# Widening the inverted softmax denominators on ScalarE instead of VectorE

## What is computed

```
x1 = x  + proj( attention( qkv(group_norm(x)) ) ) + bias          # layer 0
y  = x1 + (attention([x1, emb] Wq, [x1, emb] Wk, x1 Wv)) Wout + b # layer 1
attention: softmax(q k / 8) v  per head and image
```

## Time and profile before

| | |
|---|---|
| median of 3 runs | 4526.37 us (4523.8 to 4527.9) |
| the profiled execution: time | 4527.92 us |
| the profiled execution: span, first to last instruction | 4526.1 us |
| granted TensorE clock, mean of the span | 0.991 of full speed |
| TensorE busy | 4293.3 us, 95% |
| VectorE, ScalarE, GpSimd busy | 71%, 61%, 32% |
| one block in the steady part, 3089.54 to 3124.92 | 35.38 us, of which TensorE is busy 33.99 |

### The profile page before, as it was taken

The page is one execution under the profiler, slowest core; times in us unless marked ns, Lnnn a source line. Parts: engine busy times, 40 slices in busy tenths (PEclk is TensorE's granted clock), DMA queues, the critical chain, the costliest instruction groups (busy, mean ns, idle before and its releaser), DMA issues. The chain is left out here.

```text
span 4526.1 us, 87274 instructions
## 1 busy us (share of the span) xinstructions
PE 4293.3 (95%) x32280; PEld 2523.6 (56%) x32280; DVE 3200.0 (71%) x2892; ACT 2747.3 (61%) x2885; POOL 1455.2 (32%) x584
## 2 busy tenths in 40 slices
PE   7998999999999999998999979999999999999999
PEld 4554555555555555554555545555555555555545
DVE  4223888888888888887433348888888888888862
ACT  1112777777777777776011128777777777777750
POOL 0000444444444444444100004444444444444430
PEclk9999999999999999999999999999999999999999
DMA  5334111211112111120444441211112111111216
GB/s 196 128 128 133 24 53 33 64 33 50 42 44 54 36 47 38 49 50 30 163 149 167 139 115 26 65 33 50 42 44 53 36 47 38 49 42 45 61 32 213
DMA packets 234733, 321.69 MB, mean 71 GB/s; under 512 B 12080, under 2 KB 221104, under 8 KB 233648
## 3 DMA queue, kind: packets, MB, share of 16 engines
q1 hardware_dynamic: 214512, 292.54, 22.3%
q10 hardware_dynamic: 20160, 28.32, 1.7%
HBM read 188.69 MB, written 132.12 MB: 71 GB/s over the span
## 5 line engine op out<-in xcount | busy, mean ns | idle before, releaser
L619 POOL TENSOR_TENSOR prob<-prob,mx 128x1056 f32<-128x1056 f32 x576 | 1434.2, 2490 | 2907.7 <-DVE prob L619 2906.3
L766 ACT ACTIVATE prob<-psum_att 128x1152 f32<-128x1152 f32 x1152 | 1294.1, 1132 | 817.1 <-DVE run L851 635.2
L708 PE MATMUL psum_att<-qst,kst 128*128 128x384 f32 x6912 | 1416.7, 348 | 49.2 <-DMA kst<-qk_scratch 27.6
L779 ACT ACTIVATE prob<-prob 128x1152 f32<-128x1152 f32 x1152 | 1288.1, 1163 | 17.3 <-POOL prob L619 17.3
L708 PEld LDWEIGHTS psum_att<-qst,kst 128*128 128x128 f32 x6912 | 1182.4, 190 | 177.9 <-issue 144.8
L721 PE MATMUL psum_att<-prob,vst 128*32 128x384 f32 x13824 | 1234.2, 490 | 4.7 <-ACT prob L779 2.9
L851 DVE TENSOR_TENSOR run<-psum_att,run 128x1152 f32<-128x1152 f32 x768 | 1013.2, 1349 | 222.3 <-PE psum_att L708 222.1
L619 DVE TENSOR_TENSOR prob<-prob,mx 128x1248 f32<-128x1248 f32 x576 | 996.1, 1730 | 155.8 <-ACT mx L773 155.8
L721 PEld LDWEIGHTS psum_att<-prob,vst 128*32 128x32 f32 x13824 | 391.7, 109 | 593.4 <-issue 593.2
L730 PE MATMUL psum_att<-prob,const_sb 128*32 128x384 f32 x6912 | 663.2, 486 | 0.0
L317 PE MATMUL psum<-xc_l,wq 128*128 128x384 f32 x1536 | 505.1, 490 | 10.4 <-DVE hl_l L422 5.3
(11 more groups left out here) (55 smaller groups left out, 1498.0 us busy)
## 6 DMA issues: line engine op xcount, KB each, us to landing
qk_scratch<-hl_l SPq DMA_DIRECT2D x48, 1536.0 KB, 5.6
qst<-qk_scratch SPq DMA_DIRECT2D x192, 384.0 KB, 5.5
kst<-qk_scratch SPq DMA_DIRECT2D x192, 192.0 KB, 3.3
v_scratch<-vo_l SPq DMA_DIRECT2D x24, 768.0 KB, 3.5
vst<-v_scratch SPq DMA_DIRECT2D x96, 192.0 KB, 2.5
att_scratch<-ob ACTq DMA_DIRECT2D x96, 192.0 KB, 1.9
attc_l<-att_scratch SPq DMA_DIRECT2D x24, 768.0 KB, 5.3
x_sb<-in_x SPq DMA_DIRECT2D x8, 1152.0 KB, 14.2
```

Source lines behind the costliest of these rows:

```text
L619: return engine.tensor_tensor(x, x, m, ALU.subtract)
L708: mm = nc.tensor.matmul(psum[:, 3 * e + k, 0:CH], kst[:, e, (3 * c + k) * P:(3 * c + k + 1) * P], qst[par][:, 2 * w + e, :], start=(w == 0 ...
L766: nc.scalar.activation(chunk_of(par, c, e), s_bank(e), ACT.Copy).then_inc(copied, 1)
L779: nc.scalar.activation(x, x, ACT.Exp, scale=SCALE).then_inc(exp_done, 1)
```

## The change

The copy of the inverted denominators into `dwide` is taken from VectorE's `invert` and becomes an activation on ScalarE, `widen(t)`, which does the same (`ACT.Copy` of the operand that repeats each inverse 64 times) and signals the same semaphore. It stands at the end of ScalarE's group 2 (`DEN_TURN_AT`), behind both copies of scores and both exponentials of that group. It waits for `inverted` and, like the copy before it, for the last `spread`. The flag `POOL_BEHIND`, which was True, goes, and its wait is unconditional.

```diff
--- before.py
+++ after.py
@@ -28,7 +28,6 @@
 GN_EPS = 1e-5
 NORM_STEPS = 10
 SHIFT_DVE = 208
-POOL_BEHIND = True
 SHIFT_LAG, EXP_LAG, PV_LAG = 7, 9, 10
 PV_COLS = 32
 DEN_PAIRS = [[0], [1, 2], [3], [4, 5], [6], [7, 8]]
@@ -786,6 +785,14 @@
                 nc.scalar.activation(pvr[:, :], pv_bank, ACT.Copy).then_inc(pv_copied, 1)
                 nc.scalar.activation(den[:, :], den_bank, ACT.Copy).then_inc(den_copied, 1)
 
+            def widen(t):
+                act.wait_ge(inverted, t + 1)
+                if not before(t, 1):
+                    act.wait_ge(spread, t)
+                nc.scalar.activation(dwide.rearrange("p r (e i) -> p r e i", e=2),
+                                     dcol[:, :, :].unsqueeze(3).broadcast_to([P, 3, 2, D]), ACT.Copy)\
+                    .then_inc(widened, 1)
+
             def store(t, par):
                 pair = t // JB
                 pair_row, j_off = (pair % PAIRS) * P, (pair // PAIRS) * HW + (t % JB) * CH
@@ -807,6 +814,8 @@
                             copy_max(t - 1, 1 - par, e)
                     if live(te):
                         exponential(te, pe_, ce, 1)
+                    if c == DEN_TURN_AT and not before(t, 3) and live(t - 3):
+                        widen(t - 3)
                     if c == STORE_AT and not before(t, 3) and live(t - 3):
                         store(t - 3, 1 - par)
 
@@ -823,8 +832,7 @@
                         if c == 0:
                             pool.wait_ge(mx_ready, unit(t, 1))
                         pool.wait_ge(copied, slot(t, c, 1))
-                        if POOL_BEHIND:
-                            pool.wait_ge(dve_shifted, group(t, c))
+                        pool.wait_ge(dve_shifted, group(t, c))
                         shift_part(nc.gpsimd, par, c, SHIFT_DVE, CH).then_inc(pool_shifted, 1)
 
         @block.vector
@@ -875,11 +883,6 @@
                 if not before(t, 1):
                     dve.wait_ge(widened, t)
                 nc.vector.reciprocal(dcol[:, :, :], dsum[:, :, :]).then_inc(inverted, 1)
-                dve.wait_ge(inverted, t + 1)
-                if not before(t, 1):
-                    dve.wait_ge(spread, t)
-                nc.vector.tensor_copy(dwide.rearrange("p r (e i) -> p r e i", e=2),
-                                      dcol[:, :, :].unsqueeze(3).broadcast_to([P, 3, 2, D])).then_inc(widened, 1)
 
             def norm(t, par):
                 dve.wait_ge(spread, t + 1)
```

## The result

The changed kernel takes 4707.28 us (median of 4 runs, 4703.9 to 4708.38), the kernel before 4526.49 (4 runs). The ratio is 1.0399, with a 95% interval of 1.0381 to 1.0417: slower by 4.0%, 181 us. Forecast were 4590 and a range of 4570 to 4620. The direction was right, the size was not.

What follows compares the result with a forecast made beforehand. TensorE was taken as the bound, pausing steadily only at line 698. 90 blocks x 0.70 us gave 63 us, plus 1 us in the tails, on 4527.92 gave 4591.9, adjusted to the runs' median as 4590; range 4570 to 4620.

Steps and rivals of the forecast that it cites:

- The reading of the bound: TensorE's only steady-block wait is at line 698, 1.34 us, 90 times, caused by VectorE's `dwide` copy held by GpSimd.
- The chain: Group 2: maxima 1.95 us earlier, then ScalarE's copy, exponential and 0.52 us widening; spread starts 0.70 us later.
- the lower bound: Low end of the sum: first maximum 0.13 us sooner, widening 0.48 us, so 0.53 a block, 48 us.
- 90 x 0.70 = 63 us: Total cost of the longer pause at `spread_den`: 0.70 us more in each of 90 blocks.
- The clock: Rival: TensorE's granted clock falls behind the longer pause; 2.28 us a block, 205 us, 4731 us; chance 0.05.
- The faster rival: Widening ready when TensorE arrives at the spread, so the whole 120.8 us pause goes: 4406 us; chance 0.03.
- Held by TensorE: Rival: ScalarE's copy (2,0) really waits for TensorE's weighing; spread 2.65 us later, 239 us, 4765 us; chance 0.04.
- No change: Rival: the 0.70 us lateness is caught up within the block, 4526 us; chance 0.04.
- One expected sign: ScalarE's copies of scores should wait less for VectorE's maxima, by near 1.95 us a block.

Runs made afterwards that it cites:

- Experiment 6: Kernel with widening on ScalarE before its first group 2 score copy, plus VectorE's copy put back ahead of the maxima, result unused: 4526.24 us.
- experiment 4: Kernel before the change, with VectorE's own copy into `dwide` moved behind both maxima of group 2, nothing added on ScalarE: 4398.05 us.
- experiment 1: Changed kernel with 14 idle-work transposes on TensorE ahead of its wait for the widening: 4580.22 us, ratio 1.0122.
- experiment 7: Changed kernel with 4 idle-work transposes on TensorE ahead of its wait for the widening: 4577.54 us, ratio 1.0114.
- experiments 2: Changed kernel with the widening put on ScalarE ahead of its first copy of scores in group 2: 4397.88 us, ratio 0.9716.
- experiment 8: Kernel before the change, with an idle-work VectorE reduction ahead of the group 2 maxima to lengthen the pause: 4642.99 us, ratio 1.0260.

## Why the prediction was right in direction and wrong in size

**The reading of the bound held.** TensorE's only steady pause was at line 698, and it came from VectorE's copy, held until GpSimd had ended. Experiment 6 brings back both the copy's 2033 ns and the 4526 us; experiment 4 has the copy at 350 ns once GpSimd is out of the way. This is also what the Trainium skill (SBUF — State Buffer, "Who interferes with whom") says of a VectorE copy in a two-port mode. No row names the mode that the copy runs in; what the rows show is that it is held, and its end.

**The chain held, to 0.02 us.** Forecast was a spread later by 0.70, it is later by 0.68. Inside it two small errors cancel: the maximum starts 0.31 behind the reduction's start and not 0.43, the overlap that the lower bound had, and TensorE starts 0.15 behind the widening's end (1314.91 - 1314.76) and not 0.05. The 0.05 was read behind a copy of scores, with the wait instruction for `widened` long past; here that instruction is the last to be released. The widening took 0.512 for the 0.52 forecast. Experiments 1 and 7 show what this chain alone is worth: 4580 and 4578 us, against a forecast of 4590; with the 8 us of TensorE's sooner start added back, 4586 to 4588.

**The step that failed is the one that costed the longer pause at its own length alone,** in the forecast's words "90 x 0.70 = 63 us". The clock was set aside as a rival at 0.05, and it is what happened: 4731 was worked out for it, 4707 came. Its price per block was nearly right, 1.58 forecast and 1.50 measured: two blocks of 37.56 against the 35.38 of before are 2.18 more each, less 0.68 makes 1.50. In group 3, the scores lost 3.41 - 2.33 = 1.08 and the weighing 2.61 - 2.14 = 0.47 (2.14 in the row of experiment 1). The total is smaller than 4731, 12 us of it since eight of the 90 blocks don't have the fall, and 7 by the price. The reason given against it, that TensorE works without a gap around the pause, was no protection. The rows left the interval between 1.4 (harmless) and 2.55 (harmful) empty, and 2.09 lies in its middle; that called for even odds, and for a range up to the other case, not for 1 in 20.

**How the time falls apart:** 4707.3 - 4526.5 = 181. The longer pause 61 us; the lowered clock, from the changed kernel against experiment 7, 4707.3 - 4577.5 = 130, of which 8 belong to the wait instruction, so 122. 61 + 122 = 183, to within the runs. Counted by blocks, the clock is 82 x 1.5 = 123.

**The faster rival was the better kernel, not what was run.** The pause does go as soon as the widening is ready on TensorE's arrival: 4398 us by experiments 2 and 4, where the rival said 4406. What kept the change from it was its place behind an exponential and a copy that have nothing to do with it. **"Held by TensorE"** falls: with the maxima earlier, the copy (2,0) started 1.78 behind the reduction and not 3.84. **No change** falls: nothing caught the lateness up.

One expected sign did not come: ScalarE's waits for the maxima did not fall in total (835.3 for 635.2 us). In group 2 the wait fell from 3.62 to 1.60, but in group 3 it rose from 0.39 to 2.89 in the block shown, where ScalarE now waits for scores that are made later. A wait of an engine off the path moved; it said nothing of the end.

## What to carry to other kernels

Of a pause of TensorE, ask not only how long it gets but whether the work behind it keeps its clock: in this loop pauses of 1.0 to 1.7 us a block cost their own length, those of experiment 8, 1.9 in the mean, cost 1.5 us more in 41 of 90 blocks, and the 2.0 to 2.1 of the changed kernel did so in 82 of 90. Where the pause can't be removed, a few idle matmuls in it can be worth more than they cost: four of them took 130 us off here. An operation moved to another engine takes its lateness from all that stands ahead of it there, so put it where that engine waits anyway; and before moving it, try whether its own engine can do it later, when the neighbour that held it is done.

## What was not expected of the hardware

The clock did not fall in the pause but 1.2 us after work had resumed (0.50 granted from 1316.1, work from 1314.91; at most 1.5 us after it in all 82 blocks), and it stayed low for 3.4 us of full work. Two pauses of equal length, 1.94 us, in the same steady loop, had different results. And with useless transposes ahead of it, the wait for the widening was no instruction of its own any more, and the spread started 0.09 us sooner.
